# Windowed attention in two of four layers: where the reciprocals of a group's softmax sums stand in VectorE's order

## The reference

```
attn = einsum('bqc,bkc->bqk', q * scale, k)             # per head
attn = attn + rel_h[..., None] + rel_w[..., None, :]    # positions, from q
attn = softmax(attn)                                    # over the keys
out  = attn @ v
return out @ proj_w + proj_b
```

## Time and profile before

| | us |
|---|---|
| median of 3 runs | 586.06 |
| the three runs | 582.06, 586.06, 591.04 |
| the profiled execution's own time | 582.49 |
| its span in the profile | 580.7 |
| PE busy in the span | 505.4 |
| DVE busy | 323.1 |
| ACT busy | 225.1 |
| POOL busy | 125.1 |
| mean granted clock of PE, share of full | 0.94 |

### The profile page before, as it was taken

One profiled execution on the slowest core, in us unless ns is written; L12 is line 12 of the kernel. 1 busy time (PEld: TensorE's weight loads), 2 busy tenths in 40 slices (PEclk: granted clock), 3 DMA queues, 4 the chain that ended last, 5 costly groups with the idle time before them and its releaser, 6 DMA issues.

```text
span 580.7 us, 10371 instructions
## 1 busy us (share of the span) xinstructions
PE 505.4 (87%) x3908; PEld 411.7 (71%) x3908; DVE 323.1 (56%) x852; ACT 225.1 (39%) x441; POOL 125.1 (22%) x175
## 2 busy tenths in 40 slices
PE   7988778699987879999788999989889678999997
PEld 6657666588865778677666898848477556888577
DVE  4758776468230773666766544246696961820142
ACT  4315444616344116445232325342255544252210
POOL 5203010143004124224403016020020103120030
PEclk9999879699987989999898899999988796999999
DMA  6892444324311674574493017204706422200001
GB/s 165 208 210 58 94 94 94 112 111 109 92 54 47 154 178 106 120 188 114 102 200 127 2 26 180 50 20 110 167 2 139 94 49 97 70 1 0 1 0 56
DMA packets 22344, 55.20 MB, mean 95 GB/s; under 512 B 5026, under 2 KB 10906, under 8 KB 22166
## 3 DMA queue, kind: packets, MB, share of 16 engines
q1 hardware_dynamic: 22078, 54.43, 38.5%
q10 hardware_dynamic: 216, 0.10, 0.1%
HBM read 11.97 MB, written 0.79 MB: 22 GB/s over the span
## 4 chain that ended last, share of the span: by engine, by line
PE 64%; DVE 22%; ACT 7%; issue 3%; DMA 3%; SPq 0%; DVEq 0%; ACTq 0%
PE PS L1341 62%; DVE NM L1229 5%; ACT HT L1076 2%; DMA KA<-KHL 2%; DVE HL L1242 2%; DVE REL L1216 1%; DVE STAT L1124 1%; DVE HL L1246 1%; DVE OT L1269 1%; DVE OT L1267 1%; DMA QA<-NR 1%; PE PS L1498 1%; DVE V L1172 1%; DVE QHL L1196 1%; PE PS L1373 1%
## 5 line engine op out<-in xcount | busy, mean ns | idle before, releaser
L1229 DVE TENSOR_REDUCE NM<-PS 98x2 f32<-98x392 f32 (+2 forms) x192 | 103.7, 566 | 55.6 <-PE PS L1341 53.7
L1050 ACT ACTIVATE PT<-PS 98x392 f32<-98x392 f32 (+2 forms) x192 | 93.0, 522 | 95.0 <-PE PS L1341 92.5
L1341 PE MATMUL PS<-KA,QA 126*98 126x196 f32 (+3 forms) x432 | 92.5, 317 | 13.9 <-DVE NM L1229 7.8
L1341 PE MATMUL PS<-QA,KA 128*98 128x196 f32 (+2 forms) x480 | 92.4, 309 | 5.8 <-ACT PT L1050 3.8
L1341 PEld LDWEIGHTS PS<-KA,QA 126*98 126x98 f32 (+3 forms) x432 | 65.8, 197 | 33.5 <-issue 20.9
L1341 PEld LDWEIGHTS PS<-QA,KA 128*98 128x98 f32 (+2 forms) x480 | 76.0, 209 | 11.1 <-ACT PT L1050 5.9
L1341 PE MATMUL PS<-W,HT 128*128 128x192 f32 x288 | 48.8, 329 | 3.9 <-ACT HT L1076 3.9
L1341 PE MATMUL PS<-PT,V 128*32 128x196 f32 (+2 forms) x672 | 51.8, 359 | 0.0
L1341 PEld LDWEIGHTS PS<-W,HT 128*128 128x128 f32 x288 | 46.6, 190 | 6.1 <-ACT HT L1076 5.9
L1341 PE MATMUL PS<-XR,W 128*128 128x512 f32 x144 | 39.5, 399 | 0.1
L1341 PEld LDWEIGHTS PS<-PT,V 128*32 128x32 f32 (+2 forms) x672 | 26.0, 123 | 13.7 <-issue 1.5
(11 more groups left out here) (132 smaller groups left out, 823.8 us busy)
## 6 DMA issues: line engine op xcount, KB each, us to landing
QA<-QHL SPq DMA_DIRECT2D x36, 192.0 KB, 4.2
KA<-KHL SPq DMA_DIRECT2D x24, 228.0 KB, 4.2
QA<-REL SPq DMA_DIRECT2D x24, 224.0 KB
QA<-QHL SPq DMA_DIRECT2D x12, 384.0 KB, 4.1
KA<-KHL SPq DMA_DIRECT2D x12, 384.0 KB, 5.1
KA<-PT SPq DMA_DIRECT2D x12, 380.0 KB
QA<-REL SPq DMA_DIRECT2D x48, 64.0 KB
W1R<-in_w SPq DMA_DIRECT2D x3, 768.0 KB, 4.2
```

The costliest lines, as they stand in the source:

```text
L1050: nc.scalar.activation(dst, src, ACT.Exp).then_inc(probs_done.sem, 1)
L1229: nc.vector.tensor_reduce(dst, src, AX.X, ALU.max, negate=True).then_inc(max_done.sem, 1)
L1341: return nc.tensor.matmul(dst, lhsT, rhs, start=start, stop=stop, skip_group_check=loose)
```

## The change

Only the list of steps of layers 0 and 2 changes. The two `inverse` halves of group 0 are spread over two heads: the first stays at part 1 of head 5, the second goes from part 3 of head 5 to part 1 of head 6, and `divide` from part 5 of head 5 to part 4 of head 6. For group 1 both halves go from parts 1 and 3 of head 9 to parts 0 and 2 of head 10, and `divide` from part 5 of head 9 to part 4 of head 10. The step `weights` goes from part 1 to part 5 of head 10, so it stays behind `divide`. No instruction is added, removed or changed in form.

```diff
-    taken, turned, late = 0, ahead - 1, []
+    taken, turned, late = 0, ahead - 1, {}
...
-            out += [step for at, step in late if at == k]
+            out += late.get((h, k), [])
...
-            if (h, k) == (HEADS - 2, 1):
+            if (h, k) == (HEADS - 2, 5):
                 out.append(("weights", 0, 0, 0))
-        late = []
         if values and h % L.per_group == 0:
             g = h // L.per_group - 1
             out.append(("copy_o", g, 0, 0))
-            late = [(1, ("inverse", g, 0, 0)), (3, ("inverse", g, 1, 0)), (5, ("divide", g, 0, 0))]
+
+            first, second = ((h + 1, 1), (h + 2, 1)) if g == 0 else ((h + 2, 0), (h + 2, 2))
+            late = {first: [("inverse", g, 0, 0)], second: [("inverse", g, 1, 0)],
+                    (h + 2, 4): [("divide", g, 0, 0)]}
```

## The result

The median of 20 runs is 576.61 us (573.31 to 583.26), against 586.61 us (580.78 to 595.48) for 20 runs of the kernel before; the ratio of the changed kernel to the one before is 0.9853, with a 95% interval of 0.9824 to 0.9883. The ratio is taken over fast runs, those within 1.5% of the fastest of their kernel, so it is not quite the ratio of the two medians (0.9830). It stands for 8.6 us of 586.6, between 6.9 and 10.3; the medians lie 10.0 us apart. The forecast was a gain of 10.4 us and a median of 575.7 us: the median came 0.9 us above it, and the gain by the ratio is smaller than forecast. The profiled execution has a span of 576.2 us and took 578.04.

A forecast was written before the change was run, and what follows sets the result against it. PE sets the time and waits for DVE up to maxT 7 and maxT 11, then for `aug` 10. 2 layers x (2.3 + 2.5) = 9.6, with the clock 10.4: median 575.7 us from 586.06, range 568.5 to 583.5.

The forecast's parts named there:

- Group 0, up to maxT 7: Layer 0, heads 5 to 7: maxT 7 2.32 us earlier, 1.72 from inverse 0.1 and 0.60 from the collision.
- The collision's share: Casts of HL ahead of maxT 7, slowed beside POOL's second multiplication: 0.60 us of their 0.72 excess goes.
- the 0.12 us that I let stay: Casts of HL ahead of maxT 7: part of the 0.72 us excess expected to remain beside POOL's multiplication.
- Group 0, up to maxT 9: Heads 7 and 8: the whole 2.3 us gain arrives, DVE and DMAs coming out together; bounds 0 and 2.44.
- four maxima: DVE after the copy for maxT 8: four maxima at 0.45 us each, from 88.05 to 89.85.
- `Aug` 9: Not moved though max 9.0 comes some 1.4 us earlier; no wait expected, `aug` 10 taken as the second bound.
- Group 1: Both halves behind maxT 11, which starts 2.5 us earlier; bounds 0 and 3.43, with 5 us to spare before the projection.
- The clock in heads 10 and 11: PE's clock after the shorter wait: 0.8 us gained taken, between 3.1 gained and 1.5 lost in layer 0.
- A: Group 0 gains nothing, inverse 0.1 holding maxT 8; sign: new PE wait over 1.5 us; 581.1 us, chance 0.17.
- D: Order hardly matters as PE is behind anyway; only the collision goes, 1.2 us: 584.9 us, chance 0.05.
- B: Clock stays full through heads 10 and 11 in both layers: 12.7 us gained, 573.4 us, chance 0.14.
- Rival C: Short PE halts in heads 5 to 7 leave the clock low over head 8's `pv`: at worst 593.2 us, chance 0.04.

The follow-up runs named there:

- With PE kept busy: Changed kernel plus products nobody reads where PE would wait: two ahead of max 8.0, six ahead of max 9.0, five ahead of maxT 11; 574.90 us, ratio 0.9839.
- both further moves: Changed kernel with group 0's halves moved to head 8 and `aug` issued ahead of the row of the maxima; ratio 0.9853.
- group 1 alone: Against the kernel before, only group 1's halves moved to head 10, group 0 as before; ratio 0.9857.
- the halves in head 8: Changed kernel with group 0's inverse halves at parts 0 and 2 of head 8, beside the `pv` steps; ratio 0.9825.

## Why the prediction held, and where it was off

**What bounds it**: right. PE waited for DVE in two places a layer, and the two moves act on these alone.

**Group 0, up to maxT 7**: forecast 2.32 us earlier, measured 2.35 and 2.34 (inverse 0.0 to maxT 7 3.62 and 3.63 instead of 5.97). The collision's share was confirmed by itself, 0.61 and 0.72. The rule of the Trainium skill that was weighed there (GPSIMD Engine Reference, section 8) agrees with the casts of before as far as they go (0.96 us beside POOL, 0.24 without it), though no row shows whether a cast is one of the instructions it names, and no run has the subtraction beside POOL's multiplication. It did not come to bear in the new order: the multiplications end 0.02 us after the casts' start and cost nothing. Of the 0.12 us that I let stay, none was seen.

**Group 0, up to maxT 9**: the mis-sized term. Forecast 2.3, measured 2.01 and 1.61. The step that failed is "four maxima" at 0.45 us each after the copy for maxT 8. The price was read from the row of 89.27, which I called max 8.2 to 8.5; it is max 9.2 to 9.5, made by PE at full clock, and the row of 85.19 (2.41 us) is max 8.2 to 8.5. In the changed kernel the four took 2.41 us in both layers, as the ones of head 8 had before, because PE feeding them was at half clock again. I had taken PE's slow products as a cost that would vanish with the 2.66 us halt; it moved one head on instead, behind the new halt of 1.80 us in layer 0 and the shorter ones in layer 2. With PE kept busy the stretch is 14.02 and 14.01, so 2.36 and 2.39 us under the kernel before: the 2.3 of the forecast. The walk also disagreed a little with its own term: it ends with maxT 9 at 90.9, which is 2.1 and not 2.3 us before the 93.03 of the kernel before.

**`Aug` 9**: I saw no wait in its advance and named `aug` 10 as the second bound. In the changed kernel neither holds PE, but `aug` 9 is the nearer: the added products that need it started 7.5 us after inverse 0.0, and max 9.0 of the changed kernel starts at 7.6. With no inverses it binds.

**Group 1**: forecast 2.5, measured 2.46 and 2.47. The wait of 0.99 us for ACT stayed, as said, and set the rest. The halves ran from 108.12, POOL was done at 112.82, PE's projection began at 118.08: 5.3 us to spare, forecast 5.

**The clock in heads 10 and 11**: 0.8 us gained by forecast, 1.12 measured (+0.17 and -1.29). The clock was not kept, not even in the run with added products; the gain is layer 2's alone. I have one profile of each kernel for this term, and in the experiments it ranges from 10.4 to 12.2 us with the same work, so the 1.12 says little of the change.

**Sum**: 9.67 us in the stretches against 10.4; by the runs 8.6 (6.9 to 10.3), medians 10.0 apart. Of the signs of being wrong, A's came in part: in layer 0 PE has a new wait of 1.80 us for DVE before max 9.0, 1.07 us ahead of maxT 8, and this is A's queue on DVE. A's price did not come, as group 0 gives 1.6 to 2.0; nothing speaks for D, and B's full clock did not come. Rival C did not decide here, but the loss that it names is real: a low clock over head 8's `pv` came in the kernel without group 0's inverses (9.15 for 7.75) and with both further moves (10.38), and there it took back much of the gain. That the short halts of the new order cause it is not shown: it also came with group 1 alone (9.19), whose heads 5 to 7 are those of the kernel before.

## What to carry to other kernels

When a stall sits behind work that nobody waits for soon, moving that work behind the last item of the tight chain gives back as much of its length as the next limit allows (2.46 of 3.44 us for group 1, where ACT came next), and the sum can be done on the timeline of one engine. But walk it at the speed that the feeding engine will really have, and look at what stands ahead of the moved work's result in the next engine's queue: `weights` had to move too. Two limits one behind the other have to be lifted together. And a gain in one stretch can be lost in the next, where the engine is itself the bound and its clock is low (10.38 for 7.75 us here): look at its granted clock in the stretch after the gain.

## What the runs showed that I had not expected

The two casts of HL, 0.24 us alone, took 0.96 us when POOL's multiplication of 128x512 ran beside them and ended 0.09 us before they did; started 0.02 us before its end they took 0.24. The other overlaps fit: 0.58 us in head 11 before, 0.51 and 0.46 with the halves in head 8, each ending about 0.10 us after POOL's instruction.

Full work for PE alone did not bring the clock back at once: in the changed kernel PE was busy all of 91 to 94 at 0.50. And products whose result nobody reads paid for themselves in their own stretch: eight of them a layer, ahead of max 8.0 and 9.0, took 0.35 and 0.78 us off maxT 6 to maxT 9. The five ahead of maxT 11 did not keep the clock there.
